# Two- and four-row multiplies on GpSimd in a state-space layer: six states' B rows in pairs, C products by four states, with smaller rings and a new order

## What is computed

```python
def step(s, inp):
    d_t, u_t, B_t, C_t = inp
    dA = jnp.exp(d_t[..., None] * A)
    s = s * dA + (d_t * u_t)[..., None] * B_t[:, :, None, :]
    y_t = jnp.einsum('bhdn,bhn->bhd', s, C_t)
    return (s, y_t)
...
y = ys + x * Dskip
y = y * jax.nn.silu(z)
out = y @ out_proj_w.T
```

## Time and profile before

| | us |
|---|---|
| median of 3 runs | 4095.38 (4092.26 to 4097.22) |
| the profiled execution | 4092.62 |
| its span, first to last instruction | 4090.5 |
| 2.1 us of it lie around the span | |

### The profile page before, as it was taken

How to read it: one execution, slowest core, us unless ns; L and a number is a source line. 1 busy time by engine, 2 the same in 40 slices (tenths; PEclk the granted TensorE clock), 3 DMA queues, 4 the chain that set the end, 5 groups by cost and what they waited for, 6 DMA issues and landing times. The chain is left out here.

```text
span 4090.5 us, 68836 instructions
## 1 busy us (share of the span) xinstructions
PE 3967.5 (97%) x20652; PEld 1972.0 (48%) x20652; DVE 3967.9 (97%) x5426; ACT 3672.5 (90%) x6935; POOL 3939.0 (96%) x2461
## 2 busy tenths in 40 slices
PE   4899999999999999999999999999999999999998
PEld 1234544544544545545544545545545544544545
DVE  6999999999999999999999999999999999999994
ACT  4899999999999999999999999999999999999875
POOL 5999999999999999999999999999999999999993
PEclk8999999999999999999999999999999999999999
DMA  3666666666656665665665656655665666566560
GB/s 104 211 208 192 196 196 189 201 194 193 200 193 192 201 193 191 201 195 189 200 197 187 202 194 190 200 194 192 198 196 193 196 197 194 195 197 193 192 190 22
DMA packets 307414, 772.86 MB, mean 189 GB/s; under 512 B 37734, under 2 KB 89062, under 8 KB 307046
## 3 DMA queue, kind: packets, MB, share of 16 engines
q1 hardware_dynamic: 305616, 767.03, 58.5%
q10 hardware_dynamic: 1430, 1.44, 0.2%
HBM read 743.16 MB, written 25.17 MB: 188 GB/s over the span
## 5 line engine op out<-in xcount | busy, mean ns | idle before, releaser
L762 POOL TENSOR_TENSOR prod<-state,cs 128x1024 f32<-128x1024 f32 x1024 | 2420.4, 2370 | 45.4 <-DVE state L1008 44.1
L987 DVE TENSOR_TENSOR db<-db,du 128x512 f32<-128x512 f32 x1408 | 958.5, 681 | 25.7 <-PE db L1062 25.5
L492 ACT ACTIVATE decay<-delta,aneg 128x512 f32<-128x512 f32 x1408 | 959.6, 715 | 20.7 <-DVE state L1008 20.3
L1077 PE MATMUL ybank<-prod,ident 64*64 64x512 f32 x3584 | 883.7, 605 | 12.1 <-POOL prod L762 9.9
L1077 PE MATMUL cross<-prod,ident 64*64 64x512 f32 x3584 | 883.7, 604 | 0.0
L1008 DVE TENSOR_TENSOR_SCAN state<-decay,carry,db 128x512 f32<-128x512 f32 x704 | 874.6, 1258 | 0.0
L1008 DVE TENSOR_TENSOR_SCAN state<-decay,db 128x512 f32<-128x512 f32 x704 | 833.6, 1200 | 0.1
L753 POOL TENSOR_TENSOR brow<-brow,du 128x512 f32<-128x512 f32 x640 | 824.0, 1288 | 3.3 <-PE bank_b L1345 3.1
L1062 PE MATMUL db<-pieces,sel 128*128 128x512 bf16 x1408 | 539.9, 384 | 34.0 <-DVE state L1008 32.1
L492 ACT ACTIVATE db<-delta,aneg 128x512 f32<-128x512 f32 x640 | 439.4, 687 | 8.0 <-DVE state L1008 6.4
L1077 PEld LDWEIGHTS ybank<-prod,ident 64*64 64x64 f32 x3584 | 205.9, 132 | 422.3 <-issue 333.4
(11 more groups left out here) (150 smaller groups left out, 7663.8 us busy)
## 6 DMA issues: line engine op xcount, KB each, us to landing
cs<-c_rows SPq DMA_DIRECT2D x1024, 512.0 KB, 3.8
brow<-b_rows SPq DMA_DIRECT2D x640, 256.0 KB, 4.1
xin<-in_hidden SPq DMA_DIRECT2D x128, 128.0 KB, 3.7
xres<-in_hidden SPq DMA_DIRECT2D x128, 128.0 KB, 4.4
out_x<-ot SPq DMA_DIRECT2D x128, 128.0 KB, 3.7
c_rows<-xdbl SPq DMA_DIRECT2D x128, 32.0 KB, 1.6
b_rows<-xdbl SPq DMA_DIRECT2D x128, 32.0 KB, 1.7
win<-in_win_t SPq DMA_DIRECT2D x1, 1024.0 KB, 8.0
```

What stands on the lines that cost most here:

```text
L492: act.activation(out, delta[:, w.mod(2), :], ACT.Exp, scale=aneg[:, w.mod(HEADS), n:n + 1]).then_inc(done, 1)
L762: pool.tensor_tensor(prod[:, r, :, :], state[:, 2 * p:2 * p + 2, :], cs[:, c, :, :], ALU.mult).then_inc(weighted, 1)
L987: dve.tensor_tensor(t[:, :], t[:, :], du[:, gu % 2, :], ALU.mult).then_inc(db_done, 1)
L1077: last = pe.matmul((ybank, cross)[k][c * Q:(c + 1) * Q, :], ident[rows, rows], prod[rows, p % P_RING, k, :], start=(p == 0), stop=(k == 1 ...
```

## The change

- BY_POOL has six states, 1, 4, 7, 9, 11 and 14, in place of 1, 4, 8, 11 and 14. So PE spreads and DVE multiplies 10 rows of B in a unit, not 11, and a sixth row is copied by DMA (256 KB more in a unit).
- `drive` multiplies two rows of B at once by du, which is repeated over the two (128x1024): three instructions in a unit in place of five. The ring `brow` holds two such twos in place of three rows. A two is copied when both states of the two before the last are scanned.
- `weigh` takes four states (128x2048): four instructions in place of eight. It waits for the fourth scan. The ring `cs` holds two fours in place of three pairs, each filled by two DMAs; both wait for the weighing two fours before.
- `decay` has 5 buffers in place of 6, `uu` has 2 in place of 4. SiLU(x) waits, for its buffer, for a new semaphore `d_mm` (the matmul of the D term that reads `uu`), and for `du_done` and `xd_mm` of one unit earlier than it did.
- The slots and the order in them are chosen anew on all engines, DMA queue included. Of the FFN's roundings on DVE, one is moved over a scan (`between`).

The diff, cut to these points:

```diff
-RING = 6
+RING = 5
...
-BY_POOL = (1, 4, 8, 11, 14)
+BY_POOL = (1, 4, 7, 9, 11, 14)
 N_POOL = len(BY_POOL)
 N_DVE = NST - N_POOL
-WEIGHED_ROWS = 3
+N_TWOS = N_POOL // 2
+ROW_TWOS = 2
 
...
-PAIRS = NST // 2
-C_RING = 3
+PAIRS, QUADS = NST // 2, NST // 4
+C_RING = 2
...
-        cs = sb("cs", [C_RING, 2, CH])
-        brow = sb("brow", [WEIGHED_ROWS, CH])
+        cs = sb("cs", [C_RING, 4, CH])
+        brow = sb("brow", [ROW_TWOS, 2, CH])
         prod = sb("prod", [P_RING, 2, CH])
         delta = sb("delta", [2, CH])
         du = sb("du", [2, CH])
-        uu = sb("uu", [4, CH])
+        uu = sb("uu", [2, CH])
...
             def spread_c(u, p):
 
-                i = u.val(PAIRS, p)
+                i = u.val(QUADS, p // 2)
                 if p == 0:
                     sp.wait_ge(c_written, u.val(16, 16))
                 wait(sp, weighted, i + 1 - C_RING)
                 rows = c_rows[u.mod(2), 2 * p:2 * p + 2, :].rearrange("n c -> (n c)")
-                sp.dma_start(cs[:, i % C_RING, :, :].rearrange("p n c -> p (n c)"),
+                part = slice(p % 2 * 2, p % 2 * 2 + 2)
+                sp.dma_start(cs[:, i % C_RING, part, :].rearrange("p n c -> p (n c)"),
                              rows.unsqueeze(0).broadcast_to([P, 2 * CH])).then_inc(c_landed[i % C_RING], 16)
 
             def copy_b(u, n):
 
-                g = u.val(NST, n)
-                i = of_pool(g)
+                i = of_pool(u.val(NST, n))
+                two, which = i // 2, i % 2
+                s = two % ROW_TWOS
                 if n == BY_POOL[0]:
                     sp.wait_ge(b_written, u.val(16, 16))
-                if i >= WEIGHED_ROWS:
-                    wait(sp, scanned, ON_POOL[i - WEIGHED_ROWS] + 1)
+                if two >= ROW_TWOS:
+                    wait(sp, scanned, ON_POOL[2 * (two - ROW_TWOS) + 1] + 1)
                 row = b_rows[u.mod(2), n:n + 1, :]
-                sp.dma_start(brow[:, i % WEIGHED_ROWS, :], row.broadcast_to([P, CH])).then_inc(b_landed[i % WEIGHED_ROWS], 16)
+                sp.dma_start(brow[:, s, which, :], row.broadcast_to([P, CH])).then_inc(b_landed[s], 16)
...
+                if w := due("scan", 8):
+                    spread_c(w, 4)
+                if w := due("scan", -8):
+                    copy_b(w, 1)
...
+                if w := due("scan", 10):
+                    spread_c(w, 5)
...
+                    wait(act, y_taken, v.val(plus=-3))
+                    wait(act, d_mm, v.val(plus=-1))
+                    wait(act, du_done, v.val(plus=-1))
+                    wait(act, xd_mm, v.val(plus=-1))
+                    act.activation(uu[:, v.mod(2), :], pbank[:, :], ACT.Silu, bias=cb[:, h:h + 1]).then_inc(u_done, 1)
...
-            def drive(w, n):
-
-                g = w.val(NST, n)
-                i = of_pool(g)
-                s = i % WEIGHED_ROWS
-                wait(pool, b_landed[s], 16 * (i // WEIGHED_ROWS + 1))
+            def drive(w, k):
+
+                i = w.val(N_TWOS, k)
+                s = i % ROW_TWOS
+                wait(pool, b_landed[s], 32 * (i // ROW_TWOS + 1))
                 pool.wait_ge(du_done, w.val(plus=1))
-                pool.tensor_tensor(brow[:, s, :], brow[:, s, :], du[:, w.mod(2), :], ALU.mult).then_inc(db_pool, 1)
-
-            def weigh(w, p):
-
-                i = w.val(PAIRS, p)
-                c, r = i % C_RING, p % P_RING
-                pool.wait_ge(scanned, w.val(NST, 2 * p + 2))
-                wait(pool, c_landed[c], 16 * (i // C_RING + 1))
-                wait(pool, summed, w.val(PAIRS, p + 1 - P_RING))
-                pool.tensor_tensor(prod[:, r, :, :], state[:, 2 * p:2 * p + 2, :], cs[:, c, :, :],
-                                   ALU.mult).then_inc(weighted, 1)
+                both = du[:, w.mod(2), :].unsqueeze(1).broadcast_to([P, 2, CH])
+                pool.tensor_tensor(brow[:, s, :, :], brow[:, s, :, :], both, ALU.mult).then_inc(db_pool, 1)
+
+            def weigh(w, q):
+
+                i = w.val(QUADS, q)
+                c, r = i % C_RING, 2 * q % P_RING
+                pool.wait_ge(scanned, w.val(NST, 4 * q + 4))
+                wait(pool, c_landed[c], 32 * (i // C_RING + 1))
+                wait(pool, summed, w.val(PAIRS, 2 * q + 2 - P_RING))
+                pool.tensor_tensor(prod[:, r:r + 2, :, :].rearrange("p a b c -> p (a b) c"),
+                                   state[:, 4 * q:4 * q + 4, :], cs[:, c, :, :], ALU.mult).then_inc(weighted, 1)
...
             def between(b, j, n, due):
 
                 if t := due("post", 55):
-                    round_down_h(t, 1)
+                    round_up_h(t, 1)
...
-                        wait(dve, db_pool, i + 1)
-                        by, plus = bank_g, brow[:, i % WEIGHED_ROWS, :]
+                        wait(dve, db_pool, i // 2 + 1)
+                        by, plus = bank_g, brow[:, i // 2 % ROW_TWOS, i % 2, :]
...
-                    wait(dve, weighted, u.val(PAIRS, n // 2 + 1 - PAIRS))
+                    wait(dve, weighted, u.val(QUADS, n // 4 + 1 - QUADS))
...
-                    pe.wait_ge(weighted, w.val(PAIRS, p + 1))
+                    pe.wait_ge(weighted, w.val(QUADS, p // 2 + 1))
...
+                if w := due("scan", 21):
+                    sum_up(w, (6,))
+                if w := due("scan", 21):
+                    sum_up(w, (7,))
...
+                        last = pe.matmul(cross[others, :], ddiag[rows, w.mod(HEADS), :], uu[rows, w.mod(2), :],
+                                         start=False, stop=False, tile_position=(r * Q, (1 - r) * Q),
+                                         skip_group_check=True)
+                if w:
+                    last.then_inc(d_mm, 1)
```

More of the change, by code:

```diff
@@ L248, in build @@
         b_written = sem("b_written")
-        b_landed = [sem(f"b_landed{i}") for i in range(WEIGHED_ROWS)]
+        b_landed = [sem(f"b_landed{i}") for i in range(ROW_TWOS)]
         db_pool = sem("db_pool")
@@ L629, in step @@
+                if due("post", 37) and not due("pre", 21):
+                    act.preload_act_table_set("exp_and_others")
+                if w := due("scan", 5):
+                    decay_of(w, 7)
+                if w := due("scan", 5):
+                    decay_of(w, 8)
+                if t := due("post", 36):
+                    silu_gate(t, 0)
                 if t := due("post", 20):
@@ L687, in unit @@
+                if w := due("scan", 3):
+                    decay_of(w, 6)
+                if w := due("scan", 3):
+                    decay_of(w, 4)
             def unit(trip, j):
@@ L765, in step @@
             def step(b, j, n):
                 u, due = timetable(b, j, n)
-                if w := due("scan", 11):
-                    weigh(w, 4)
+                if w := due("scan", 7):
+                    weigh(w, 0)
+                if w := due("scan", 13):
+                    weigh(w, 2)
+                if t := due("post", 23):
+                    pool.wait_ge(v_scale, t.val(3, 3))
+                    pool.tensor_tensor(blocks(v2), blocks(v2), spread(vs[:, 3, :], DM // BLK),
+                                       ALU.mult).then_inc(v_norm, 1)
@@ L1277, in side @@
-                if v := due("pre", 20):
-                    pe.wait_ge(mid_done, v.val(plus=1))
-                    pe.matmul(pbank[:, :], less[:, 1, :], mid[:, :], start=False, stop=True,
-                              skip_group_check=True).then_inc(res_mm, 1)
-                if t := due("post", 29):
-                    pe.wait_ge(v_quant, t.val(plus=1))
-                    if peeled and t.val() == 0:
-                        pe.wait_ge(xnt_done, 11)
-                    else:
-                        wait(pe, h_op, t.val(2))
-                    for k in range(KM):
-                        last = pe.transpose(bank_b[:, k * P:(k + 1) * P], v2_eps[:, k * P:(k + 1) * P], ident[:, :])
-                    last.then_inc(v_tp, 1)
```

567 lines of the change are left out of this document (268 added, 299 removed).

## The result

The changed kernel takes **4105.89 us** in the median (4098.86 to 4111.55), the kernel before 4094.20 in the same comparison (4092.00 to 4097.22): ratio 1.0026, 95% interval 1.0016 to 1.0035. It is slower, by 0.16 to 0.35%; forecast was 4092.4 and no change. The profiled execution has a span of 4102.4 us, 11.9 more than before.

What follows compares the result with a forecast made beforehand. DVE and PE bound the kernel, POOL nearly full. Late units losing 0.02 us and early ones 0.03 gave 3 us: span 4090.5 to 4087.5, plus 2.1 and 2.8, 4092.4 (no change); range 4068 to 4130.

Steps and rivals of the forecast that it cites:

- POOL's work: POOL's multiplies of a unit: own work rises by 0.25 to 30.67 us (30.54 to 30.80), making it the fullest engine.
- fours at that price: POOL's 128x2048 products at the skill's 4497 ns: some 0.05 us cheaper each, about 4 us off the forecast.
- Rival 3: POOL's two- and four-row multiplies save no beginnings: 32.6 us a unit, 4331; chance 0.06 together with other waits.
- The wait for state 12: DVE's multiply for state 12 waits for PE's spread: 0.58 us in late units, 0.98 in early ones.
- Taking the larger of the two bounds for each kind of unit: Unit length: late units at DVE's work plus wait, 30.87 us; early ones at POOL's 30.67, above DVE's 30.58.
- the landing: L, time for the DMA of the third four's second half to land: 3.8 us median, 7.0 at most before.
- rival 2's loop: C rows late behind the copy waiting for scan 9, a loop over two units; 4118 to 4149 us, chance 0.22.
- the deciding point: Landing time from which the two-unit loop through the C-row DMA sets the pace: 4.4 us.
- The price of rival 2: Cost of late C rows: 26 us more at a landing of 5.0 us (4118), 57 more at 5.5 (4149).
- the prediction's formula: Two-unit loop through the C-row DMA: 57.3 us plus landing; each us of landing above 4.4 adds 0.5 a unit.
- Start and end at nothing: The 153 us outside whole units, at the run's start and end: no change, 3 us either way.

Runs made afterwards that it cites:

- e1_c5: Changed kernel with the DMA for pair 5's C rows issued ahead of the copy that waits for scan 9: 4088.1 us, ratio 0.9990 to the kernel before.
- run 15: Not a label of a run: part of the phrase "the run 15 to 18 us", by which the changed kernel's time is longer than that of e1_c5.
- f3_dose: Changed kernel with one wait more, the DMA for pair 5's C rows also waiting for scan 10: 4113.0 us, ratio 1.0045 to the kernel before.

## Why the prediction was wrong

**POOL's work: right.** 30.67 was forecast, and POOL takes 30.64 to 30.70 in six of the eight units of a trip of e1_c5. A four is busy for 4554 ns, as forecast (4.53 to 4.57). By starts it takes 4.49 us in the median (4.50 in the row at 2007.90), where the straight line had 4.52; the 4497 ns of the Trainium skill ("GPSIMD Engine Reference", "Performance versus the Vector engine") agree with this case by starts and are 1% below it by busy time. (The prediction's "about 4 us" for fours at that price should be 6 by its own bounds: early units 30.58 and not 30.67, 64 times.) Rival 3 is out.

**The wait for state 12: right.** 0.50 and 0.99 in e1_c5, forecast 0.58 and 0.98. Late units take 30.92 (30.87), early ones 30.48 (30.58 before POOL was taken into account).

**Taking the larger of the two bounds for each kind of unit: slightly wrong.** POOL does not go at DVE's pace in late units and at its own in early ones. It takes about 30.67 in six of the eight units of a trip, never idle, and 30.8 to 30.9 in the other two; it lags behind DVE in the early ones, and the buffers carry that to the next late unit. The trip is then not 4 x 30.87 + 4 x 30.67 = 246.16 but 245.77 (e1_c5), 3 to 4 us less a run of this term, or 0.16 above the 245.61 of DVE and PE alone.

**The step that failed: the landing, and with it rival 2's loop put at nothing.** The prediction wrote "L was 3.8 in the median and 7.0 at most, and this DMA now has two of 256 KB around it", set the deciding point at 4.4, left the loop out of the forecast and gave the case a chance of 0.22. The 3.8 is the median of all C-row DMAs of the kernel before, of a queue in which one was issued each time that a pair was done. In the changed kernel the DMA behind the copy lands after 4.34 us in the median (3.70 before) and after up to 5.30, above 4.6 in 30 of its 128 cases. POOL waits ahead of that product in 34 of the 112 units of the middle, a trip is 0.80 us longer than with the DMA ahead of the copy, and the run 15 to 18 us (after against e1_c5; 12.6 in the middle of the profiled executions). The change itself reorders this queue and so had to move this number: it was read from the one place where it could not hold. And it was used as one number, where the loop takes its cost from the long landings and not from the median. Without the late rows, e1_c5 says, the forecast would have been 4 us too high, on the other side.

**The price of rival 2: the loop right, its use wrong.** 57.3 and the landing was forecast for two late units, 57.2 and the landing is measured. For a landing that is always the same the prediction's formula gives nothing at 4.34, the median of this DMA. At 4.8, the median of all, it gives 31.05 for late units and nothing for early ones, 0.09 a unit or 12 us. Measured are 0.10 a unit, 12.6 us in the middle, but this agreement is luck: the 4.8 belongs to other DMAs. Of the 0.80 a trip, 0.39 are left when POOL has time to spare, from single long landings; the other half comes from POOL being full, which the formula did not have.

**Start and end at nothing, "3 us either way": wrong.** After against before they make +5.2 (-2.0, +4.4, +2.8), e1_c5 against before -1.0 (-5.1, +2.5, +1.5). The start's part in these sums (+2.4 and -2.6) is within its scatter. But all 13 kernels with the change take 120.9 to 124.4 to the first L959 and 137.2 to 142.9 for the five units, where the one profiled execution of the kernel before has 126.2 and 134.7, so both seem to have moved. In the first units, in which there is no feed-forward work, DVE waits for PE's spreads as it does later, and PE in turn for a four, with a spread behind it. The timeline of the changed kernel, third unit:

```profile
167.49 1.12 PE L1072 MATMUL ybank<-prod,ident 64*64 64x512 f32 x2 [2.17 <-POOL prod L769]
...
170.47 0.70 DVE L982 TENSOR_TENSOR db<-db,du 128x512 f32<-128x512 f32 x1 [2.17 <-PE db L1057]
```

The granted clock of PE (the column ahead of the last two), a mean over its levels of 1.2 and 2.4 GHz, is 0.90 and 0.89 there, where the kernel before has 0.99 and 1.00:

```profile
120.00:150.00 30.00, 25.69 (x121) 7.62 (x117) 26.91 (x30) 24.40 (x42) 28.72 (x11) 0.90 0.62 209
150.00:180.00 30.00, 24.17 (x114) 6.99 (x115) 25.79 (x29) 23.36 (x41) 28.40 (x10) 0.89 0.64 205
```

How much of the 4.4 is the wait and how much the clock is open; the lower clock is not needed for it, since in f3_dose's five units it is 1.00 and they take 139.3. Cutting the fours did not bring it back.

## What to carry to other kernels

When a change reorders a DMA queue, the landing time read from the kernel before is not a constant to put into the sum: price it as an unknown that the change moves, look at the landings of the one DMA on the path and at the long ones among them, not at the median of its line, and look for each transfer that stands in the queue behind one that waits for a late event. Put it ahead of that one; here this was worth 15 to 18 us and turned the change from 0.26% slower to 0.1% faster. Where three engines are full within 0.2%, a wait of one is not a gain to be had: the spread for state 12 moved 2 us ahead cost 81 and 96 us, moved 0.95 ahead gained nothing, and moved in one kind of unit alone gained 5.

## What the runs showed of the hardware

- The same DMA of 512 KB lands after 3.8 us in the median in the kernel before and 4.8 in the changed one, with 806 MB moved in place of 773. More than on the kernel it depends on the place in the queue. Of the eight C-row DMAs of a unit of the changed kernel, the three that SP issues with no other in the 3 us before them land after 3.5 to 3.7 us in the median. The four with three to five others in the 3 us before them take 5.0 to 7.0, and the one behind the copy, with one, 4.34. That the others are the cause was not tried by itself.
- GpSimd's multiply takes 2.12 ns for each element more, by the medians of the starts ((4.49 - 2.32) / 1024), where the second operand is read in full, but 1.72 where it is a scale repeated over 16 elements: 1.35 us for 704 elements against 0.44 for 176 ((1.35 - 0.44) / 528). Timeline of POOL, full and cut:

```profile
2001.43 1.38 POOL L795 TENSOR_TENSOR hh<-hh,hs 128x704 f32<-128x704 f32 x1
2002.78 2.35 POOL L760 TENSOR_TENSOR brow<-brow,du 128x1024 f32<-128x1024 f32 x1
2005.10 4.52 POOL L769 TENSOR_TENSOR prod<-state,cs 128x2048 f32<-128x2048 f32 x1
```

```profile
1982.71 0.48 POOL L795 TENSOR_TENSOR hh<-hh,hs 128x176 f32<-128x176 f32 x1
1983.15 2.36 POOL L760 TENSOR_TENSOR brow<-brow,du 128x1024 f32<-128x1024 f32 x1
```

- After PE had stood 2.17 us for a product, two matmuls that take 0.65 us elsewhere took 1.12, with the granted clock of the stretch at 0.89. There PE lost more than the wait's own length. That the wait brought the clock down is not shown: in e1_c5 PE stood for 2.37 us at 166.5 to 168.8 and the clock stayed at 1.00.
